# Six attention layers and a gated network on one core: one maximum for each pair of score banks, all other products in one bank, two of four relus moved to VectorE

## The reference

```
q, k = h @ wq.T + bq, h @ wk.T + bk              # 16 heads of 8
scores = einsum("blhd,bmhd->bhlm", q, k) / sqrt(8)
w_avg  = softmax(scores).mean(over the 16 heads)
new_w  = softmax(w_avg + rel)                    # rel = exp(-|i-j| / 16)
h1 = ln(h + new_w @ h);  h2 = ln(h1)
out = ln(h2 + relu(h2 @ w1.T + b1) @ w2.T + b2)  # 128 -> 512 -> 128
```

## Time and profile before

| | |
|---|---|
| runs | 2649.18, 2652.36, 2653.47 us; median 2652.36 |
| span of the profiled execution | 2651.5 us (no other time of that execution is given) |
| PE, DVE, ACT, POOL busy | 2528.1, 2414.4, 2422.1, 1516.9 us |
| first exponential starts | 34.15 us |
| last exponential starts | 2362.81 us |
| granted TensorE clock, mean | 0.995 |

### The profile page before, as it was taken

How to read it: one execution, slowest core, us unless ns; L and a number is a source line. 1 busy time by engine, 2 the same in 40 slices (tenths; PEclk the granted TensorE clock), 3 DMA queues, 4 the chain that set the end, 5 groups by cost and what they waited for, 6 DMA issues and landing times. The chain is left out here.

```text
span 2651.5 us, 89129 instructions
## 1 busy us (share of the span) xinstructions
PE 2528.1 (95%) x35384; PEld 1185.5 (45%) x35384; DVE 2414.4 (91%) x5440; ACT 2422.1 (91%) x6760; POOL 1516.9 (57%) x1846
## 2 busy tenths in 40 slices
PE   5999999999999999999999999999999999999999
PEld 1344444444444444444444444444444344346887
DVE  6999999999999999999999999999999999984433
ACT  5999999999999999999999999999999999983232
POOL 3568856566566565664665655656656655544211
PEclk8999999999999999999999999999999999999999
DMA  4122222211212112122112122121121221200000
GB/s 132 58 77 68 74 71 71 66 46 54 69 42 84 57 54 63 49 70 66 46 60 64 46 84 68 54 64 48 54 83 44 65 62 38 66 19 5 28 17 24
DMA packets 98913, 152.87 MB, mean 58 GB/s; under 512 B 17856, under 2 KB 81088, under 8 KB 88896
## 3 DMA queue, kind: packets, MB, share of 16 engines
q1 hardware_dynamic: 97936, 146.26, 18.4%
q10 hardware_dynamic: 560, 0.92, 0.1%
HBM read 92.58 MB, written 41.94 MB: 51 GB/s over the span
## 5 line engine op out<-in xcount | busy, mean ns | idle before, releaser
L932 ACT ACTIVATE ex<-sc,negmax 128x512 f32<-128x512 f32 x3072 | 2125.0, 833 | 12.8 <-DVE negmax L729 8.9
L729 DVE TENSOR_REDUCE negmax<-sc 128x1 f32<-128x512 f32 x3072 | 1922.0, 673 | 18.1 <-PE sc L1064 12.8
L1064 PE MATMUL sc<-kb,qb 96*32 96x512 bf16 x12288 | 1077.2, 385 | 85.5 <-ACT ex L932 62.5
L932 ACT ACTIVATION_READ_ACCUMULATOR ex<-sc,negmax 128x1 f32 x3072 | 1082.8, 352 | 0.0
L1082 PE MATMUL mean<-ex,rw 128*32 128x512 f32 x6144 | 796.2, 593 | 7.5 <-ACT ew L938 7.5
L1064 PEld LDWEIGHTS sc<-kb,qb 96*32 96x32 bf16 x12288 | 319.9, 94 | 1005.8 <-ACT ex L932 883.4
L545 POOL TENSOR_TENSOR rw<-sel_sb,zinv 128x256 f32<-128x256 f32 x384 | 236.4, 616 | 661.8 <-DVE zinv L735 661.5
L1082 PEld LDWEIGHTS mean<-ex,rw 128*32 128x32 f32 x6144 | 186.5, 110 | 151.9 <-issue 72.8
L1071 PE MATMUL m<-hc,pt 128*32 128x129 f32 x6144 | 206.8, 275 | 0.0
L1071 PE MATMUL m<-h2t,w_sb 128*32 128x512 f32 x1536 | 201.5, 597 | 2.4 <-ACT relu L983 2.4
L1071 PE MATMUL m<-w_sb,relu 128*32 128x128 f32 x6144 | 201.3, 273 | 0.0
(11 more groups left out here) (124 smaller groups left out, 2425.5 us busy)
## 6 DMA issues: line engine op xcount, KB each, us to landing
kb<-qk_split SPq DMA_DIRECT2D x288, 128.0 KB
qb<-qk_split SPq DMA_DIRECT2D x568, 64.0 KB
qk_split<-kp SPq DMA_DIRECT2D x144, 128.0 KB, 1.9
qk_split<-qp SPq DMA_DIRECT2D x141, 128.0 KB, 1.8
hc<-hs SPq DMA_DIRECT2D x48, 256.0 KB, 2.8
xin<-x SPq DMA_DIRECT2D x16, 256.0 KB, 3.2
fh_raw<-fh SPq DMA_DIRECT2D x2, 1024.0 KB, 5.4
y_kept<-xin SPq DMA_DIRECT2D x8, 256.0 KB, 2.0
```

The source lines that it names most:

```text
L729: nc.vector.tensor_reduce(negmax[:, s % RT:s % RT + 1], sc[s % NS][:, :], AX, ALU.max, negate=True) \
L932: nc.scalar.activation(ex[:, s % ET, :], sc[s % NS][:, :], ACT.Exp, bias=negmax[:, c:c + 1], accum_out=zsum[:, c:c + 1]).then_inc(exp_read ...
L1064: ins = nc.tensor.matmul(sc[s % NS][h * QS:h * QS + QS, :], qb[t % 2][:, h % 2, g, h // 2, r:r + QS], kb[t % 2][:, g, h // 2, :], start=Tr ...
```

## The change

Five things change together.

- The six score banks are one tensor of six banks (`NS` = 6). `score_max` runs in odd slots only, waits for both tiles of a pair, reads two banks in one instruction (128 x 2 x 512) and writes two columns of `negmax`. The exponentials stay one for each tile.
- `m0` is gone. The transposes of the mean and the attention product go to `m1` with all else but the head sums, and `m1_read` waits for the readers of both.
- Relus 1 and 3 of each unit are done by VectorE as `tensor_scalar` (add the bias, maximum with 0); 0 and 2 stay with ScalarE.
- At the start and in the network at the end, score bank 5 takes the place of `m0`.
- Nearly all entries of `STEP` are new, those of the network at the end too.

The core of the diff (of the table, the entries that the prediction speaks of):

```diff
@@ -15,7 +15,7 @@
-NS = 5
+NS = 6
...
@@ -43,70 +43,70 @@ STEP = {
-    "invert_sums": (12, 17, 25, 36, 42, 55, 57, 66),
-    "row_weights": (18, 20, 30, 45, 48, 56, 66, 75),
-    "sum_heads": (21, 23, 25, 26, 32, 33, 45, 50, 52, 56, 61, 64, 69, 71, 74, 75),
-    "exp_mean": (25, 47, 63, 73),
-    "transpose_mean": (30, 54, 68, 79),
-    "relative": (30, 56, 73, 78),
-    "attend": (40, 59, 76, 82),
-    "residual": (40, 64, 76, 81),
-    "spread": (83, 98, 176),
-    "stats1": (94, 94, 94, 94),
-    "up": (147, 150, 156, 158),
-    "relu": (145, 150, 153, 158),
-    "down": (163, 165, 170, 172),
-    "add": (172,),
-    "stats2": (173, 174, 174, 174),
-    "last_turn": (204,),
-    "head_square": (75, 85, 86, 93, 94, 97, 111, 114, 118, 119, 129, 133, 142, 146, 159, 208),
+    "invert_sums": (16, 22, 27, 36, 46, 50, 62, 72),
+    "row_weights": (5, 8, 15, 31, 44, 51, 57, 62),
+    "sum_heads": (19, 21, 25, 29, 32, 34, 40, 50, 53, 56, 57, 61, 67, 73, 76, 77),
+    "exp_mean": (26, 47, 61, 75),
+    "transpose_mean": (33, 59, 75, 82),
+    "relative": (33, 59, 75, 81),
+    "attend": (42, 66, 80, 88),
+    "residual": (42, 66, 80, 88),
+    "spread": (92, 113, 181),
+    "stats1": (104, 108, 108, 108),
+    "up": (155, 159, 163, 167),
+    "relu": (153, 160, 161, 167),
+    "down": (173, 173, 175, 177),
+    "add": (177,),
+    "stats2": (178, 179, 179, 180),
+    "last_turn": (230,),
+    "head_square": (120, 133, 154, 155, 160, 163, 168, 193, 233, 240, 282, 317, 332, 333, 372, 467),
...
@@ -157,6 +157,8 @@
+
+RELU_ACT, RELU_DVE = (0, 2), (1, 3)
@@ -259,11 +261,11 @@
-        sc = [ctx.enter_context(nc.psum_tensor(f"sc{i}", [P, S], f32)) for i in range(NS)]
+        scores = ctx.enter_context(nc.psum_tensor("scores", [P, NS, S], f32))
+        sc = [scores[:, i, :] for i in range(NS)]
-        m0 = ctx.enter_context(nc.psum_tensor("m0", [P, S], f32))
-        first_banks, value_banks, square_banks, out_banks = (sc[1], sc[2]), (sc[3], sc[4]), (sc[0], mean), (m0, m1)
+        first_banks, value_banks, square_banks, out_banks = (sc[1], sc[2]), (sc[3], sc[4]), (sc[0], mean), (sc[5], m1)
@@ -725,9 +727,9 @@
             def score_max(t, j):
                 s = t * TILES + j
-                dve.wait_ge(scores_ready, s + 1)
-                nc.vector.tensor_reduce(negmax[:, s % RT:s % RT + 1], sc[s % NS][:, :], AX, ALU.max, negate=True) \
-                    .then_inc(max_ready, 1)
+                dve.wait_ge(scores_ready, s + 2)
+                nc.vector.tensor_reduce(negmax[:, s % RT:s % RT + 2], scores[:, s % NS:s % NS + 2, :], AX, ALU.max, negate=True) \
+                    .then_inc(max_ready, 2)
...
@@ -816,8 +818,8 @@
-                if g < U:
-                    score_max(g, j)
+                if g < U and j % 2:
+                    score_max(g, j - 1)
@@ -838,6 +840,13 @@
+                for c in RELU_DVE:
+                    for t in due("relu", c, g, j):
+                        dve.wait_ge(layer_loaded[RUN[t] % 2], 64 * (RUN[t] // 2) + 64)
+                        dve.wait_ge(up_ready, t * CH + c + 1)
+                        wait_later(dve, down_ready, t * NT)
+                        nc.vector.tensor_scalar(relu[:, c, :], m1[:, :], col[RUN[t] % 2][:, C_B1 + c:C_B1 + c + 1], 0.0,
+                                                ALU.add, ALU.max).then_inc(relu_ready, 1)
@@ -976,7 +985,7 @@
-                for c in range(CH):
+                for c in RELU_ACT:
...
@@ -1039,13 +1048,10 @@
                     held[name] = count
                     pe.wait_ge(what, count)
 
-            def m0_read():
-                once("qf", qf_ready, PRE)
+            def m1_read():
+                assert put["down"] % NT == 0
                 once("pt", pt_ready, put["turned"])
                 once("res", res_ready, put["attended"])
-
-            def m1_read():
-                assert put["down"] % NT == 0
                 once("h2t", h2t_ready, put["in2"])
                 once("relu", relu_ready, put["up"])
                 once("added", added, put["down"] // NT)
@@ -1059,6 +1065,8 @@
                 wait_later(pe, exp_ready, s - NS + 1)
+                if s == NS - 1:
+                    once("qf", qf_ready, PRE)
...
@@ -1085,18 +1093,18 @@
 
             def transpose_mean(t, i):
                 once("ew", ew_ready, t * NT + i + 1)
-                m0_read()
+                m1_read()
                 for c in range(NT):
-                    ins = nc.tensor.transpose(m0[:, c * P:c * P + P], ew[:, i % 2, c * P:c * P + P], id_sb[:, :])
+                    ins = nc.tensor.transpose(m1[:, c * P:c * P + P], ew[:, i % 2, c * P:c * P + P], id_sb[:, :])
                 ins.then_inc(ewt_ready, 1)
```

More of the change, by code:

```diff
@@ L59 @@
-    "norm1_bias": (87,),
-    "stats1": (94, 94, 94, 94),
[L61 to L65, removed]
-    "up": (147, 150, 156, 158),
-    "relu": (145, 150, 153, 158),
-    "down": (163, 165, 170, 172),
-    "add": (172,),
-    "stats2": (173, 174, 174, 174),
[L71 to L87, removed]
-    "last_turn": (204,),
[L89 to L94, removed]
@@ new lines @@
+    "stats0": (76, 80, 84, 90),
+    "spread": (92, 113, 181),
+    "power": (88, 112, 179),
+    "apply0": (84, 92),
+    "norm1_weight": (93,),
+    "norm1_bias": (95,),
+    "stats1": (104, 108, 108, 108),
+    "apply1": (113, 113),
+    "norm2_turn": (148,),
+    "norm2_out": (145,),
+    "token_weight": (119,),
+    "token_bias": (166,),
+    "up": (155, 159, 163, 167),
[3 more added lines that the diff above has]
+    "stats2": (178, 179, 179, 180),
@@ new lines @@
+    "apply2": (180, 182),
+    "norm3_turn": (195,),
+    "norm3_out": (196,),
+    "norm3_weight": (182,),
+    "norm3_bias": (186,),
+    "project": (199, 205),
+    "queries": (200,),
+    "keys": (203,),
+    "split_q": (209, 225, 225, 227),
+    "split_k": (199, 203, 213, 228),
+    "last_weight": (182,),
+    "last_bias": (185,),
+    "last_add": (189,),
+    "last_stats": (197,),
+    "last_spread": (202,),
+    "last_power": (199,),
+    "last_apply": (214,),
+    "last_turn": (230,),
+    "last_keep": (226,),
@@ new lines @@
+    "first_stats": (1, 3, 8, 11),
+    "first_spread": (14,),
+    "first_power": (10,),
+    "first_apply": (7, 12),
+    "first_turn": (52,),
+    "first_out": (47,),
+    "first_token": (14,),
+    "first_project": (53, 63),
+    "first_queries": (56,),
+    "first_keys": (60,),
+    "first_split_q": (55, 58, 58, 60),
+    "first_split_k": (60, 62, 67, 67),
+    "head_high": (15, 15, 39, 39, 41, 63, 63, 67),
+    "head_low": (34, 36, 44, 46, 68, 76, 76, 76),
+    "head_first": (73, 84, 98, 100, 106, 138, 144, 153),
@@ L110 @@
+    "head_silu": (65, 85, 95, 100, 118, 118, 141, 150),
+    "head_gate": (87, 90, 96, 108, 122, 123, 148, 153),
+    "head_square": (120, 133, 154, 155, 160, 163, 168, 193, 233, 240, 282, 317, 332, 333, 372, 467),
+    "head_gelu": (123, 149, 153, 153, 163, 177, 319, 349, 351, 370, 371, 387, 421, 426, 476, 488),
+    "head_split": (162, 162, 162, 174, 188, 232, 306, 338),
 }
@@ L701, in queries @@
             def queries(n):
-                nc.vector.tensor_scalar(qf[:, :], (m0 if n < PRE else m1)[:, :], bqk_sb[LAYER_OF[n] % 2][:, 0:1], DH ** -0.5,
+                nc.vector.tensor_scalar(qf[:, :], sc[5] if n < PRE else m1[:, :], bqk_sb[LAYER_OF[n] % 2][:, 0:1], DH ** -0.5,
                                         ALU.add, ALU.mult).then_inc(qf_ready, 1)
@@ L1028, in _ @@
                 wait_later(pe, qf_ready, b)
-                nc.tensor.matmul(m0[:, :], wqk_sb[0][:, 0, :], h3t[:, :], start=True, stop=True).then_inc(q_ready, 1)
+                nc.tensor.matmul(sc[5], wqk_sb[0][:, 0, :], h3t[:, :], start=True, stop=True).then_inc(q_ready, 1)
                 wait_later(pe, kf_ready, b)
```

28 lines of the change are left out of this document (5 added, 23 removed).

## The result

The changed kernel takes 2691.42 us (median of 4 runs, 2690.61 to 2693.31), the kernel before on the same chip 2652.37: a ratio of 1.0147 [1.0133, 1.0162], 39 us more where I had forecast 25 less. The profiled execution took 2693.31 us for a span of 2691.4.

A forecast was written before the change was run, and what follows sets the result against it. ScalarE was taken as the bound: 47.30 us a unit plus 0.55 of waiting gives 47.85, 28 us less over 48 units; 2651.5 - 28 + 3 = 2626.5, median 2627 us, range 2600 to 2672 (forecast's own 2614 to 2642).

The forecast's parts named there:

- What bounds the kernel, and each engine's own work: In the 48 units ScalarE bounds; two relus fewer give 47.30 us a unit, VectorE 46.9, TensorE 43.8 before.
- What the wait for a pair costs: Even tiles' exponentials wait 0.5 us longer way; VectorE's worst burst, slots 32 to 55, is 0.35 us late each unit.
- One bank `m1`: Tight place is relu 1 before the transposes in slot 33; 0.35 to 0.8 us a unit, taken as 0.55.
- many places of idle time on ScalarE: Sign of a wrong prediction; forecast was about 0.5 us idle a unit, before even exponentials in slots 34 to 55.
- The sum by engine: Bursts against ScalarE's time: VectorE 18.8 against 18.47 us, TensorE 7.5 against 7.2, the latter's lateness not added.
- The reserve of 0.4 us between VectorE's unit and ScalarE's: Per unit, VectorE's forecast 46.9 us lies 0.4 below ScalarE's 47.30.
- Most readers stand several slots ahead of the next writer.: In the single product bank, TensorE's waits cost only where a pair becomes late; the tight place is relu 1.
- The rival that ended on the slow side: VectorE becomes the bound at 48.8 us a unit, a pair costing 1.184 us: 2670 to 2690 us, chance 0.22.
- Its deciding point: VectorE sets the unit from 1.173 us for a pair, 0.05 above the forecast's value.
- Ramp and end: First exponential unchanged; in the end network `up` products of units 46 and 47 wait for readers: -3 to +8, taken +3 us.
- LOAD: Theory behind the experiments' expectations: VectorE's work, pair maxima and relus, makes the maxima late.
- BANK: Theory behind the experiments' expectations: the single product bank and the new order make the scores late.

The follow-up runs named there:

- the same three moved entries: Head sum 7, `norm2_turn` and `norm2_out` moved in the changed kernel's table: 2742.24 us with full maxima, 2636.81 us with maxima over 256 of 512 columns.
- control: Kernel before, two product banks kept, seven table entries moved so that one bank would be free of deadlock: 2771.76 us, 1.0456.
- light VectorE: Changed kernel with maxima over 256 of 512 columns: 2657.04 us in pairs, 2661.37 us with one maximum for each tile.
- equal load: For the pair: changed kernel with single maxima over 480 columns, as long as 32 full pairs: 2723.81 us, 1.0277.
- light maxima: Changed kernel, maxima over 256 columns: for the sixth bank, single maxima, six score banks 2661.37 us, five 2764.30; for the 5 us, pairs, 2657.04.
- half maxima: Changed kernel with each pair maximum reading only 256 of the 512 columns of its two banks: 2657.04 us, 1.0011.
- moved steps and half maxima: Changed kernel with maxima over 256 columns and head sum 7, `norm2_turn` and `norm2_out` moved in the table: 2636.81 us, 0.9947.

## Why the prediction failed, point by point

**What bounds the kernel, and each engine's own work: right.** ScalarE's work is 47.05 us a unit. The 47.30 of the forecast is the old unit less the relus (1.14, as forecast) and so still holds the old 0.27 us of waiting. TensorE's list adds up to 43.6 us, not 43.8; nothing hangs on it. A pair costs 1.12 us in step and 1.211 in the record (1.124 and about 1.20 forecast); the relu 0.742 in the record. VectorE is busy 483 of 500 us, 47.4 us of a unit (46.9 forecast). The Trainium skill (VectorE: DVE Perf Modes, the section on the TRN2 errata), by which a pair would save 0.125 us, was off as the row had said: 2 x 0.592 - 1.12 = 0.06.

**"What the wait for a pair costs" and "One bank `m1`": the steps that failed.** I took 0.55 us of new waiting in a unit. It is 2.06 - 0.27 = 1.79 us, 1.25 more: 1.25 x 48 = 60 us of the 64 by which the forecast missed. The prediction had named many places of idle time on ScalarE as a sign of being wrong; there are eight. It fell in three parts.

*The sum by engine.* I added up each engine's burst against ScalarE's time, with TensorE's and VectorE's lateness "in the same place, so not added", and named slots 32 to 55 as the worst. The place was right. But VectorE's burst only fits if it may start early, on scores that are there, and by the rows above TensorE does not have them there, because its own steps wait for VectorE's and ScalarE's readers one by one: VectorE stands 0.8 us just ahead of the burst. The reserve of 0.4 us between VectorE's unit and ScalarE's was an average, and it was not there either: VectorE is busy 47.4 us and ScalarE works 47.05. The late waits measure 1.3 us where I had said 0.35 to 0.8. That load and order act together is shown: the same three moved entries win 18 or lose 51 us, by the load. That the order acts through the chain is argued.

*"Most readers stand several slots ahead of the next writer."* I counted distance in slots. It was true on paper, and the trace shows five steps in a row each starting within 0.05 to 0.28 us of the end of the reader before, with TensorE standing some 0.9 us ahead of four of them. A slot is not a time where an engine runs behind.

*The early waits.* 0.72 us at tiles 8 to 18 I did not reckon at all: ScalarE waits there for a burst of VectorE around `queries` (tile 8), for maxima behind TensorE's wait for `kf` (tile 16) and for `norm2_turn` (tile 18). The forecast took the in-order engine at the bound as one for which others wait; it also has readers of its own that can be early.

**The rival that ended on the slow side** gave 2670 to 2690 us, and its last sentence (late places add up instead of sharing one) is near what happened. Its deciding point, a pair over 1.173 us, was wrong: the pair is 1.12.

**Ramp and end: the size at its bound, the cause named at most a part.** +8 us, where I took +3 of -3 to +8. TensorE idles 9.8 us from 2400 to 2500, 3.4 in the same stretch before. The cause named was `up` products that wait for readers. Such waits are there:

```profile
2404.27 0.66 PE L1098 MATMUL m<-id_sb,ew 128*128 128x128 f32 x4 [1.39 <-ACT ew L947]
...
2449.31 1.06 PE L1079 MATMUL m<-h2t,w_sb 128*32 128x512 f32 x8 [1.64 <-DVE relu L848]
```

But behind the last exponential TensorE's waits for relus come to 2.4 us (1.6 and 0.8), and they came to 2.4 before too. What is new is 2.7 us ahead of a group of `net_square`, 3.4 for the `exp_mean` of the last units, 1.4 for a copy of the last layer's result out of `m1` (L975), and 1.5 for `relative` and `residual`, which read `m0` before. Nor is the bank the only thing that lengthens the end: with two product banks and the old order, one relu on VectorE (and `head_gate` three slots later) gives an end of 293.3 us and two give 295.1, against 288.7. In the old table the single bank adds 4.8 us over its control. Which part holds here is open.

**What the parts are worth, as far as shown.** The pair: no loss with light VectorE, 32 us better at equal load. The sixth score bank: needed by this table, 103 us with light maxima. The relus on VectorE: both versions with them back are slower by some 57 us or more, but in the kernel before two cost 9 us and one wins 13. VectorE's load at the edge: 34 of the 39 us. Of the rest, 5 us with light maxima, the profile shows one: a unit of 48.31 against 48.44 us (1.14 won on ScalarE, waits of 1.25 in place of 0.27) is 6 us less over 48 units, and the end is 6.6 us longer. The profiled execution was one of its fastest (2654.18 of 2653.98 to 2657.84); the other 3 us lie in executions of which there is no trace.

**The two theories.** LOAD named what 34 us hang on, but by itself it does not say why relief from an equal load was worth 3 us before; ScalarE's own work, then 0.7 us above VectorE's, is a part of it that these runs do not size. With two relus moved in the old order VectorE does set the unit. BANK named the waits that half maxima leave (18 and 48), yet a wait at 18 is there with two product banks, and the one at 48 was a head sum's slot. Neither alone holds: the late places come with the order, and the load decides what they cost.

**What stays open.** The price of the single product bank in the changed kernel at full load. All eight banks are in use, so a second one costs a score bank, and 103 us hide the answer. That it needs the chain is argued from the rows; the 5 us with light maxima and the 311 us in the old order show only that the price lies in the table. How much of the 1.3 us belongs to the chain, how much to where the burst was put and how much to VectorE being level with ScalarE was not parted either.

## What to carry to other kernels

Sum an engine's work alone only to find a bound; for the waits, follow the chain across engines, reader by writer, and ask at each burst whether the engine may start it early. Where one bank or buffer serves many producers, count its turns in time, not in slots.

A hand-set order fits one arrangement: moving a reader to another engine, or a few entries of the table, cost 9 to 335 us here, mostly far more than the operation moved. And the move that paid, 0.46%, was the smallest: one operation of the full engine into an idle gap of 0.8 us that the profile showed on the next one.

## What the runs showed of the hardware

**The granted clock falls inside a unit.** In the control of the old table TensorE's clock, mean 0.978, is not low for one long stretch but for a short one in most units, behind its waits. Windows in two units that follow each other, and one `attend` in the first:

```profile
1020.00:1030.00 10.00, 8.45 (x181) 6.12 (x177) 7.28 (x18) 8.72 (x26) 6.31 (x8) 0.83 0.01 2
...
1075.00:1080.00 5.00, 4.75 (x108) 3.92 (x112) 3.28 (x7) 4.32 (x14) 2.50 (x4) 0.67 0.02 5
```

```profile
1022.84 0.40 PE L1064 MATMUL sc<-kb,qb 96*32 96x512 bf16 x4 [0.27 <-ACT ex L932]
1023.51 0.47 PE L1064 MATMUL sc<-kb,qb 96*32 96x512 bf16 x4 [0.27 <-ACT ex L932]
1023.75 1.95 PE L1071 MATMUL m<-hc,pt 128*32 128x129 f32 x32
1025.47 0.65 PE L1064 MATMUL sc<-kb,qb 96*32 96x512 bf16 x4
```

The `attend` takes 1.72 us, against 0.89 in the earlier trace rows, as at the lower of the two levels, 1.2 GHz. TensorE had stood 0.48 us once and 0.27 us before each of four tiles, and then has its burst at half speed. So a wait is paid twice, and the units say what the second payment is. From unit 8 on about three units of four have such a stretch and take 51.4 to 52.0 us each; the others have none and take 50.1 to 50.6. At 1.5 us for each of some 28 units that is about 42 of the control's 121 us, an estimate. The Trainium skill (TensorE: Matmul & The Clock Gate, the section on HAM oscillation) tells of a kernel whose idle time, there in waits for transfers, brings the clock down again at each step. The trace agrees that the clock comes down again and again, and here the waits are for another engine and last under 0.5 us each. With the relus back on ScalarE in unchanged slots the mean was 0.951, the lowest of all.

**A queued instruction's record grows.** The exponentials of the changed kernel read 0.68 us behind a wait (at 1033.16), 0.80 at 1044.16, and 0.69 again behind the wait at tile 40 (1049.75), though between waits they start 0.66 us apart throughout. So the mean tells how rarely ScalarE waited, and not what an exponential costs: from 600 to 1100 us it is 826 ns before, 717 here, and 741 in the kernel with moved steps and half maxima, which is faster than either. Only starts, or ends, tell the cost.
